# The gains of the state recurrence: exponential taken after the spread over the partitions, and the spread moved ahead of a projection

## The reference

```python
x = L0_attn_x                              # (16, 1024, 512)
xn = _layernorm(x, axis=-1)
x = x + _L0_attn_ref(xn, ...) + _L0_ffn_ref(xn, ...)

# _L0_attn_ref: H = 16 heads, P = 32, N = 16 states, K = 64 tokens in a chunk
proj = x @ W_in.T                          # x part, z, B, C, dt_low
dt = jax.nn.softplus(dt_low @ dt_W.T + dt_b)
dA = dtc * A
dAcs = jnp.cumsum(dA, axis=2)
Lm = jnp.exp(dAcs[:, :, :, None, :] - dAcs[:, :, None, :, :])      # causal part
scores = jnp.einsum('bcihn,bcjhn->bcijh', Cc, Bc) * Lm * dtc[:, :, None, :, :]
y_intra = jnp.einsum('bcijh,bcjhp->bcihp', scores, xc)
wx = (dtc * decay_to_end)[..., None] * xc
chunk_state = jnp.einsum('bckhn,bckhp->bchnp', Bc, wx)
chunk_decay = jnp.exp(dAcs[:, :, -1, :])
# over the chunks: h = chunk_decay * h + chunk_state
y_cross = jnp.einsum('bcthn,bchnp,bcth->bcthp', Cc, h_states, jnp.exp(dAcs))
y = y_intra + y_cross + xp * D_param
y = y / rms * norm_w * jax.nn.silu(z)
return y @ W_out.T
```

## Time and profile before

| | |
|---|---|
| median of 3 runs | 3116.52 us (3114.46 to 3118.19) |
| profiled execution | 3114.46 us |
| its span | 3112.5 us |
| mean granted TensorE clock | 0.987 |
| TensorE busy (matmul) | 2937.4 us, 94% |
| TensorE weight loads | 2514.9 us, 81% |
| VectorE busy | 2466.5 us, 79% |
| ScalarE busy | 1592.4 us, 51% |
| GpSimd busy | 1294.8 us, 42% |

### The profile page before, as it was taken

How to read it: one execution, slowest core, us unless ns; L and a number is a source line. 1 busy time by engine, 2 the same in 40 slices (tenths; PEclk the granted TensorE clock), 3 DMA queues, 4 the chain that set the end, 5 groups by cost and what they waited for, 6 DMA issues and landing times.

```text
span 3112.5 us, 134679 instructions
## 1 busy us (share of the span) xinstructions
PE 2937.4 (94%) x59784; PEld 2514.9 (81%) x59784; DVE 2466.5 (79%) x3546; ACT 1592.4 (51%) x3614; POOL 1294.8 (42%) x2029
## 2 busy tenths in 40 slices
PE   7999999999999999999999999997777777999999
PEld 5888888888888888888888888885666666888887
DVE  5899899998998999989899989885444446777775
ACT  4555555555555555555555555553333322555555
POOL 3565665655656556556565565562000010000000
PEclk9999999999999999999999999998999997999999
DMA  3211111111111111111111111115344445778765
GB/s 114 79 55 48 55 52 55 55 45 59 51 48 56 51 55 53 47 57 54 48 56 51 54 50 51 56 38 205 109 121 117 112 116 153 229 212 232 226 204 157
DMA packets 336546, 286.94 MB, mean 92 GB/s; under 512 B 52304, under 2 KB 265808, under 8 KB 335072
## 3 DMA queue, kind: packets, MB, share of 16 engines
q1 hardware_dynamic: 335392, 278.16, 30.0%
q10 hardware_dynamic: 576, 0.17, 0.0%
HBM read 165.01 MB, written 113.25 MB: 89 GB/s over the span
## 4 chain that ended last, share of the span: by engine, by line
PE 74%; DVE 17%; issue 5%; DMA 2%; POOL 1%; SPq 1%; DVEq 0%; ACT 0%; POOLq 0%; ACTq 0%
PE a_proj L811 30%; PE s_rt L1462 8%; PE a_mix L811 7%; PE g_pick_ps L1223 5%; PE s_w_ps L1448 5%; DVE scan_in L673 4%; PE a_scan L931 4%; DVE xs L691 4%; PE s_sum L1475 4%; DVE g_picked L1192 3%; PE a_scan L908 2%; PE g_acc_ps L1244 2%; PE a_scan L895 2%; PE a_mix L819 2%; PE a_mix L883 1%
## 5 line engine op out<-in xcount | busy, mean ns | idle before, releaser
L691 DVE TENSOR_SCALAR xs<-gs,mg 64x128 f32<-64x128 f32 x960 | 600.2, 684 | 8.8
L811 PE MATMUL a_proj<-wdh,xnTh 128*128 128x512 f32 x1024 | 419.3, 409 | 0.8 <-DVE wdl L627 0.8
L1418 DVE TENSOR_TENSOR s_resT<-s_w_ps,s_b 128x2048 f32<-128x2048 f32 x128 | 293.3, 2292 | 155.8 <-PE s_w_ps L1448 155.8
L1412 ACT COPY s_res<-s_rt 128x512 f32<-128x512 f32 x512 | 263.2, 600 | 291.1 <-PE s_rt L1462 291.1
L811 PE MATMUL a_proj<-wdh,xnTl 128*128 128x512 f32 x1024 | 402.5, 393 | 0.0
L811 PE MATMUL a_proj<-wdl,xnTh 128*128 128x512 f32 x1024 | 400.9, 391 | 0.0
L673 DVE COPY_PREDICATED scan_in<-mask,a_scan 64x512 f32<-64x512 uint32 x512 | 377.6, 738 | 16.0
L382 POOL TENSOR_TENSOR yv<-yt,dx 128x512 f32<-128x512 f32 x128 | 166.5, 1301 | 439.0 <-DVE yt L699 439.0
L1192 DVE COPY g_picked<-g_pick_ps 128x1024 f32<-128x1024 f32 x128 | 156.8, 1225 | 225.6 <-PE g_pick_ps L1223 225.6
L374 POOL TENSOR_TENSOR dx<-xs,d_row 64x512 f32<-64x512 f32 x256 | 329.0, 1285 | 15.1
L540 ACT ACTIVATE scan_in<-CT,hsel 64x128 f32<-64x128 f32 x1024 | 325.8, 387 | 4.8
(11 more groups left out here) (121 smaller groups left out, 6855.1 us busy)
## 6 DMA issues: line engine op xcount, KB each, us to landing
x<-in_x_dram SPq DMA_DIRECT2D x128, 256.0 KB, 3.4
xn_dram<-xn SPq DMA_DIRECT2D x128, 256.0 KB, 2.4
part_dram<-res SPq DMA_DIRECT2D x128, 256.0 KB, 2.9
g_xn<-xn_dram SPq DMA_DIRECT2D x128, 256.0 KB, 2.9
s_w<-in_w_dram SPq DMA_DIRECT2D x128, 256.0 KB, 3.8
s_part<-part_dram SPq DMA_DIRECT2D x128, 256.0 KB, 3.7
out_dram<-s_out SPq DMA_DIRECT2D x128, 256.0 KB, 3.0
g_w<-in_w_dram SPq DMA_DIRECT2D x4, 2048.0 KB, 12.7
```

Of the source, the lines that this page charges most:

```text
L691: nc.vector.tensor_scalar(dst, gs[rows_, q, :].unsqueeze(1).to_broadcast([CH, 2, 2 * HD]), scale0[rows_, q, :], scale1[rows_, q, :], ALU.m ...
L811: last = nc.tensor.matmul(out, lhs[a], rhs[c], start=(k == 0 and n == 0), stop=(k == nk - 1 and n == 2))
L1412: nc.scalar.copy(res[:, n % 4, :, :], rt_bank[n % 3][:].rearrange("p (n d) -> p n d", n=GPT)).then_inc(res_cp, 1)
L1418: nc.vector.tensor_tensor(resT[m % 2][:, :, sets].rearrange("p n (q r) -> p n q r", r=4), w2_bank[:].rearrange("p r q n -> p n q r"), b2[: ...
```

## The change

Three things change, all in the attention phase. The exponential moves: ScalarE now copies the raw sums to `logs` (L591), TensorE spreads them as they are, and ScalarE takes Exp of the 128x32 that come out, where it copied them before. spread_gains moves on TensorE, from behind the scores of tile n1+1 to between transpose_xn and project_x. And the step that makes `mg` moves on ScalarE, from between spread_c and the copy of C to ahead of the first silu (L600), along with its two waits. A wait of the old L592 on the previous stage's spread is left out.

```diff
                 nc.scalar.activation(e2[:], u, ACT.Exp, scale=-1.0).then_inc(small_cp, 1)
-                wait(act, mg_ps, s)
-                nc.scalar.activation(logs[0:H, :], misc[0:H, LOGS:LOGS + 8], ACT.Exp).then_inc(small_cp, 1)
+                nc.scalar.copy(logs[0:H, :], misc[0:H, LOGS:LOGS + 8]).then_inc(small_cp, 1)
             if s == 0:
                 stage_hi(LAST_STAGE)
 
             if valid(s + 1):
                 hi_xn(2 * (s + 1) + 1, 1 - par, 1)
             if valid(s):
+                act.wait_ge(mg_ps, s + 1)
+                wait(act, st_add, 4 * (s - 1))
+                nc.scalar.activation(mg[:, par, :, :], misc[:, GAINS:GAINS + 8 * NG].rearrange("p (g c) -> p g c", g=NG),
+                                     ACT.Exp).then_inc(mg_ready, 1)
                 silu_z(n0)
                 copy_x(n0 + 1)
...
                 spread_c(n1 + 1)
             if valid(s):
-                act.wait_ge(mg_ps, s + 1)
-                wait(act, st_add, 4 * (s - 1))
-                nc.scalar.copy(mg[:, par, :, :], misc[:, GAINS:GAINS + 8 * NG].rearrange("p (g c) -> p g c", g=NG)).then_inc(mg_ready, 1)
                 copy_c(s)
                 silu_z(n0 + 1)
...
                 transpose_xn(n0 + 3, 1)
             if valid(s):
+                spread_gains(s)
                 project_x(n0 + 1)
...
                 scores(n1 + 1)
             if valid(s):
-                spread_gains(s)
                 project_c(s)
                 project_z(n0 + 1)
```

## The result

| | before | after |
|---|---|---|
| median of 4 runs | 3115.49 us (3111.72 to 3118.19) | 3138.48 us (3133.24 to 3152.62) |
| profiled execution | 3114.46 us | 3142.84 us |
| its span | 3112.5 us | 3140.9 us |

The ratio after to before is 1.0076, with a 95% interval of 1.0052 to 1.0098: the changed kernel is slower by 23 us. I had forecast 3117.5 us and a range of 3112 to 3123. The prediction was wrong.

What follows compares the result with a forecast made beforehand. VectorE's loop (32.73 us in three stages of four) was taken to set the pace. The terms 0 + 0.5 + 0.5 + 0 = +1.0 us took the median from 3116.52 to 3117.5 us, range 3112 to 3123.

Steps and rivals of the forecast that it cites:

- Step 1: On ScalarE, logs made by a Copy of 16x8 instead of an Exp: 0, within 0.05 us either way.
- Step 2: On TensorE, spread_gains at its new place: entry 0.12 us dearer, mostly hidden by VectorE's loop; +0.5 us in all.
- Step 3: TensorE's work between new and old place comes 0.49 us later, delaying ygh for VectorE's L711: +0.5 us in all.
- Step 4: On ScalarE, the Exp of mg (0.19 us) ahead of silu does not wait and is covered by idle time: 0.
- Rival A: TensorE becomes the bound through the extra entry at the spread's new place: slower, 3127 us at the upper bound; chance 0.12.
- TensorE waits at L949: At the spread on TensorE: no wait expected after stage 0; a wait there would show the forecast wrong.

Runs made afterwards that it cites:

- exp_old_place: The kernel before, with only the exponential moved behind the spread and all places kept: 3108.06 us, ratio 0.9997.
- behind_x: The kernel before, with the spread moved on TensorE alone, to behind project_x: 3113.92 us, ratio 0.9997.
- behind_scan: The kernel before, with the spread moved on TensorE alone, to directly behind the scan and ahead of the token transposes: 3154.27 us, ratio 1.0125.
- pe_only: The kernel before, with the spread moved on TensorE alone to ahead of project_x, ScalarE unchanged: 3132.91 us, ratio 1.008.
- shift28: The changed kernel, with 7 more small matmuls (28 instructions) ahead of the first stage: 3145.45 us, ratio 1.0103.
- padded_new: The changed kernel, from the second stage on with 4 of 16 spread matmuls plus 4 longer ones into unused columns: 3122.91 us, ratio 1.003.
- quarter_new: The changed kernel, with 12 of the 16 spread matmuls left out from the second stage on: 3106.92 us, ratio 0.9995.
- full_new: The changed kernel, with the spread as 4 matmuls over the whole array in place of 16 over quarters: 3121.68 us, ratio 1.0046.

## Why the prediction was wrong

It was wrong by one thing that it left out, not by the terms that it held. Step by step:

- Step 1, the Exp and Copy of logs, 0 us: right (exp_old_place). The Copy of 16x8 takes 0.138 us, 0.012 less than the Exp:

```profile
L591 ACT COPY logs<-a_misc x64: 138/138/141, 35.4 to 2121.5; 16x8 f32<-16x8 f32 x64
```

- Step 2 is the one that failed. Its steady part was somewhat short: the entry costs 0.18 us and not 0.12 (0.59 beside 0.41), just above the upper bound of 0.17. That it would be hidden by VectorE's longer loop was right: 46 rounds are no longer than before, and behind_x with 0.12 us more per round is level with the kernel before. What failed is its last part, which asks whether TensorE can be held up at the new place and puts that at nothing. I looked for data that could be missing (logs, with 1.3 us of room), and there was enough room; I did not look at the instructions themselves. The rows were there: 128 scan matmuls in 1.3 us, each with its load of weights, then the transposes, and then 32 more of these pairs. In the kernel before, project_x broke this run. The sum lacked 13 stops of 1.25 to 2.07 us (19.4 us), and four stretches at the lower clock behind them: 2.27 us in each of twelve rounds, 27 us, where the sum had +0.5 for this step.
- Step 3: in most ordinary rounds right. L711 waits for ygh often (58 times; "in most stages" was forecast), and the distance L640 to L673 stays within 0.07 us in 39 of the 46. In the twelve rounds with a stop L711 starts 1.75 to 3.69 us after L640, and L673 comes 0.3 to 0.8 us later than it would, as the extreme case of the earlier trace rows had shown in kind.
- Step 4: right in ordinary rounds; all 13 waits of L600 are behind stops.
- Rival A gave a time that is near (3127), by another mechanism: the drain at a switch of tile shape. The Trainium skill's rule (TensorEngine Tiling (Array Packing), Tiling Modes) fits the 0.18 us of entry, and behind_scan, where a switch less makes the shortest round 0.13 us shorter. Not every switch has such a price here: the one from 32x64 to 128x32 at the old place cost 0.01 us. And the switches do not make the kernel slow: behind_scan has the fewest of them and is the slowest. That its time came near is luck: its chance of 0.12 stood for the right sign with the wrong cause.
- The prediction named "TensorE waits at L949" as what would show it wrong. That is what happened.

Shown by the runs: that the loss is TensorE's alone (pe_only), that it sits in every fifth round, that it hangs on the place in the stream (shift28) and on what stands just ahead of it (behind_x against behind_scan), and not on the tile switch (behind_scan). Shown by the counts: that the stops stand where a block of 256 instructions begins, and end 2.16 to 3.03 us after that block's transfer started. padded_new, quarter_new and full_new agree, but change the length of the run and the places of the blocks together. Open: when a block's transfer is started, and what decides that a stop is followed by the lower clock. It follows some stops and not others of like length (at 298 us behind 1.51, not at 797 behind 1.68).

## What to carry to other kernels

Where an engine runs through hundreds of short instructions in a us or two, its instructions can run out before its data do. Count instructions, not only time, when small ones are moved: 64 of them, 0.37 us long, cost nothing behind slow matmuls and 23 us behind a scan and four transposes. A stop that returns with a fixed period of rounds and has "issue" as its releaser is the mark of it, and comparing the lengths of the rounds by that period tells in one table how much of a change it explains.

## What was unexpected

- Behind a stop of 1.4 to 2.7 us on TensorE the clock can be at 1.2 GHz for 3.4 us, during which 512-column matmuls follow at 0.42 us and not at 0.23. In the attention phase between 80 and 2110 us the kernel before has no such stretch, the changed one five (17 us; the fifth, at 1691 us, stands behind a wait of 1.77 us for the masked scores), behind_scan eleven (38 us).
- Eight passes of 128x128 weights with 8 columns take 0.81 us, 32 passes of 128x32 take 0.37: four tiles side by side are more than twice as fast, but bring four times the instructions.
- A steady 0.51 us more of TensorE work per round cost at most 0.22 us per round (14 us of 33, two stops among them), and 0.12 to 0.18 us cost nothing measurable, as one would expect where VectorE's loop is the longer one.
